# A decoder with cross-attention on one core: the context's low parts and the residual input by adding DMA transfers, and each slot's context projection moved to the front of its step

## The reference

```python
# x: 16 x 112 x 256 (from the first part), y = ctx_1024: 16 x 375 x 256, H = 16 heads of D = 16
q = softmax(_heads(x @ Wq.T + bq), axis=-1)
k = softmax(_heads(y @ Wk.T + bk), axis=-1)
v = _heads(y @ Wv.T + bv)
k_cumsum = sum(k, axis=-2, keepdims=True)
D_inv = 1.0 / sum(q * k_cumsum, axis=-1, keepdims=True)
kv = einsum('bhnd,bhne->bhde', k, v)
out = q + einsum('bhnd,bhde->bhne', q, kv) * D_inv
out = out.transpose(0, 2, 1, 3).reshape(x.shape[0], x.shape[1], C)
return out @ Wp.T + bp
# around it:
x = _layernorm(x + L0_attn(x, ...))      # first part; this sum is what the attention part begins with
x = _layernorm(x + L0_xattn(x, ctx_1024, ...))
x = _layernorm(x + L0_ffn(x, ...))
```

## Time and profile before

| | |
|---|---|
| Median of 3 runs | 1837.98 us (1837.52 to 1838.78) |
| The profiled execution's own time | 1839.21 us |
| Its span in the profile | 1837.5 us |
| Busy: PE, DVE, ACT, POOL | 1736.6 us (95%), 1242.6 (68%), 977.0 (53%), 3.6 |
| Attention part | from about 700 us to about 905 us |
| PE busy, and TensorE clock granted, 700 to 718 us | 14.39 of 18.00 us, 0.87 |
| the same, 718 to 743.4 | 22.28 of 25.40 us, 0.77 |
| the same, 743.4 to 792 | 45.40 of 48.60 us, 0.99 |
| the same, 792 to 836.4 | 39.47 of 44.40 us, 1.00 |
| the same, 836.4 to 872.9 | 33.13 of 36.50 us, 1.00 |

### The profile page before, as it was taken

One profiled execution on the slowest core, in us unless ns is written; L12 is line 12 of the kernel. 1 busy time (PEld: TensorE's weight loads), 2 busy tenths in 40 slices (PEclk: granted clock), 3 DMA queues, 4 the chain that ended last, 5 costly groups with the idle time before them and its releaser, 6 DMA issues.

```text
span 1837.5 us, 27225 instructions
## 1 busy us (share of the span) xinstructions
PE 1736.6 (95%) x10508; PEld 1520.3 (83%) x10508; DVE 1242.6 (68%) x1918; ACT 977.0 (53%) x1505; POOL 3.6 (0%) x26
## 2 busy tenths in 40 slices
PE   3599999999999998998999999999999999999997
PEld 1378888778888788888899889998999989999896
DVE  7999999999999855888554445444454544445446
ACT  4688898898989773444533333333333332333323
POOL 0000000000000000000000000000000000000000
PEclk9799999999999998999999999999999999999999
DMA  4000010001000002111111010000011001120001
GB/s 143 1 25 17 12 47 18 7 8 62 1 12 29 0 30 89 44 55 45 55 35 35 1 35 35 34 33 2 34 34 34 11 23 34 34 74 0 1 1 41
DMA packets 34702, 56.59 MB, mean 31 GB/s; under 512 B 3030, under 2 KB 20412, under 8 KB 33596
## 3 DMA queue, kind: packets, MB, share of 16 engines
q1 hardware_dynamic: 34620, 55.47, 9.3%
HBM read 51.79 MB, written 3.67 MB: 30 GB/s over the span
## 4 chain that ended last, share of the span: by engine, by line
PE 70%; DVE 24%; ACT 3%; issue 2%; DMA 0%; SPq 0%; ACTq 0%; DVEq 0%
PE fbank L1935 33%; PE fbank L1957 17%; PE pair L839 5%; PE pair L799 4%; PE pair L824 3%; DVE kfl L421 2%; PE proj L1429 2%; PE pair L809 2%; DVE st L268 2%; DVE aa L370 1%; DVE bb L366 1%; DVE pp L352 1%; PE qbanks L1465 1%; PE pair L789 1%; DVE x L409 1%
## 5 line engine op out<-in xcount | busy, mean ns | idle before, releaser
L1757 DVE TENSOR_TENSOR hf<-sil,fbank 128x512 f32<-128x512 f32 (+1 forms) x256 | 158.8, 620 | 479.2 <-PE fbank L1935 407.5
L1862 ACT ACTIVATE sil<-fbank 128x512 f32<-128x512 f32 (+1 forms) x256 | 139.2, 544 | 615.1 <-PE fbank L1935 615.1
L1935 PE MATMUL fbank<-xh,wh 128*128 128x512 f32 (+1 forms) x1024 | 289.8, 364 | 1.2 <-ACT sil L1862 1.2
L1935 PE MATMUL fbank<-xl,wh 128*128 128x512 f32 (+1 forms) x1024 | 289.0, 363 | 0.0
L1935 PE MATMUL fbank<-xh,wl 128*128 128x512 f32 (+1 forms) x1024 | 288.9, 363 | 0.0
L1957 PE MATMUL fbank<-wl,hh 128*128 128x256 f32 x896 | 250.3, 279 | 0.0
L1957 PE MATMUL fbank<-wh,hh 128*128 128x256 f32 x896 | 250.2, 279 | 0.0
L1957 PE MATMUL fbank<-wh,hl 128*128 128x256 f32 x896 | 250.1, 279 | 0.0
L1935 PEld LDWEIGHTS fbank<-xl,wh 128*128 128x128 f32 x1024 | 184.6, 189 | 30.8
L1935 PEld LDWEIGHTS fbank<-xh,wl 128*128 128x128 f32 x1024 | 184.4, 189 | 30.4
L1935 PEld LDWEIGHTS fbank<-xh,wh 128*128 128x128 f32 x1024 | 180.5, 189 | 27.8 <-ACT sil L1862 1.6
(11 more groups left out here) (239 smaller groups left out, 3109.6 us busy)
## 6 DMA issues: line engine op xcount, KB each, us to landing
raw<-in_w_gate SPq DMA_DIRECT2D x16, 512.0 KB, 3.8
raw<-in_w_up SPq DMA_DIRECT2D x16, 512.0 KB, 4.7
raw<-in_w_down SPq DMA_DIRECT2D x16, 512.0 KB, 5.7
raw<-in_w_ck SPq DMA_DIRECT2D x4, 1024.0 KB, 4.8
raw<-in_w_cv SPq DMA_DIRECT2D x4, 1024.0 KB, 4.8
raw<-in_ctx_t SPq DMA_DIRECT2D x4, 750.0 KB, 5.9
ct<-in_ctx_t SPq DMA_DIRECT2D x4, 750.0 KB, 4.9
x<-in_x SPq DMA_DIRECT2D x4, 448.0 KB, 6.9
```

Source lines behind the costliest of these rows:

```text
L1757: dve.tensor_tensor(hf[i][:, 0:w], sil[i][:, 0:w], banks(e, t, f)[1][:, 0:w], ALU.mult).then_inc(hf_ready, 1)
L1862: act.activation(sil[f % 2][:, 0:w], banks(e, t, f)[0][:, 0:w], ACT.Silu).then_inc(sil_ready, 1)
L1935: ins = pe.matmul(banks(e, t, f)[k][:, 0:w], m[h][:, o:o + P], a[:, b, columns(c)], start=i == 0, stop=i == 3 * CB - 1)
```

## The change

- `ctl` is no longer made by DVE. ACT, behind each `high_context`, writes minus the high part into `ctl` (scale −1.0), and POOL issues a DMA transfer that adds the slot's context from device memory to it (`accum_op=ALU.add`). PE waits for that transfer (`ctl_in`).
- `add_input` on DVE is gone with the buffers `xin`. POOL issues four transfers that add the input to `x` in place; DVE's `input_stats` waits for them and takes the statistics.
- On PE, `project` is cut into `project_values` and `project_rest`. Both stand at the front of each step, ahead of the query projection, the output projection and the turns; the by-head products of `attend` stand between them at i = 0.
- On DVE at i = 0, `denominators` and `rsqrt` stand ahead of `k_normalise`.
- SP's next context load waits for `cth_ready` (the high part) in place of the low part. `kvbd` takes the place in memory that `xin` had.

```diff
@@ gpsimd (new) @@
+            def add_context(s):
+                pool.wait_ge(minus_ready, s + 1)
+                if s >= 2:
+                    pool.wait_ge(ctl_in[s % 2], 16 * (s // 2))
+                pool.dma_start(ctl[s % 2][:, :, 0:S], io["ctx_t"][:, :, s * S:(s + 1) * S].bitcast(F32R),
+                               accum_op=ALU.add).then_inc(ctl_in[s % 2], 16)
+            def add_input(c):
+                if c >= 2:
+                    pool.wait_ge(sum_in[c % 2], 16 * (c // 2))
+                pool.dma_start(x[:, c * G:(c + 1) * G, :], xv[:, c * G:(c + 1) * G, :], accum_op=ALU.add)\
+                    .then_inc(sum_in[c % 2], 16)
+            add_context(0)
+            add_context(1)
+            pool.wait_ge(g["x_done"], 2 * STEPS)
+            add_input(0)
+            for s in range(2, B):
+                add_context(s)
+                if s % 2 == 0 and s // 2 < GROUPS:
+                    add_input(s // 2)
@@ sync @@
-            load_x(0)
-            load_x(1)
...
-                sp.wait_ge(ctl_ready, CG * (j - 1))
+                sp.wait_ge(cth_ready, CG * (j - 1))
                 load_context(sp, io, ct, ct_in, j)
-                if j * CG % G == 0 and j * CG // G >= 2:
-                    c = j * CG // G
-                    sp.wait_ge(sum_done, c - 1)
-                    load_x(c)
@@ vector @@
-            def low_context(s):
-                c0 = (s % CG) * S
-                dve.wait_ge(cth_ready, s + 1)
-                if s >= 2:
-                    dve.wait_ge(proj_done, s - 1)
-                dve.tensor_tensor(ctl[s % 2][:, :, 0:S], ct[s // CG % 2][:, :, c0:c0 + S], cth[s % 2][:, :, 0:S],
-                                  ALU.subtract).then_inc(ctl_ready, 1)
...
-            def add_input(c):
-                dve.wait_ge(xin_in[c % 2], 16 * (c // 2 + 1))
-                dve.tensor_tensor(chunk(c), chunk(c), xin[c % 2][:], ALU.add).then_inc(sum_done, 1)
-                dve.wait_ge(sum_done, c + 1)
+            def input_stats(c):
+                dve.wait_ge(sum_in[c % 2], 16 * (c // 2 + 1))
                 stats(1, c)
...
                     if i == 0 and c1 is not None:
-                        add_input(c1)
+                        input_stats(c1)
+                    if i == 0 and c2 is not None:
+                        denominators(c2)
+                    if i == 0 and c1 is not None:
+                        rsqrt(1, c1)
...
                     k_normalise(n)
-                    if n + 2 < B:
-                        low_context(n + 2)
-                    if i == 0 and c1 is not None:
-                        rsqrt(1, c1)
-                    if i == 0 and c2 is not None:
-                        denominators(c2)
@@ scalar, high_context @@
                 act.activation(cth[s % 2][:, :, 0:S], ct[s // CG % 2][:, :, c0:c0 + S], ACT.Copy).then_inc(cth_ready, 1)
+                act.wait_ge(cth_ready, s + 1)
+                act.activation(ctl[s % 2][:, :, 0:S], cth[s % 2][:, :, 0:S], ACT.Copy, scale=-1.0).then_inc(minus_ready, 1)
@@ tensor @@
             for n in range(B):
                 i, c1, c2 = stage(n)
+                if n + 1 < B:
+                    project_values(n + 1)
+                if i == 0 and c2 is not None:
+                    attend(c2)
+                if n + 1 < B:
+                    project_rest(n + 1)
                 if i == 1 and c1 is not None:
                     pe.wait_ge(xt_ready, c1 + 1)
                     tokens_out(qbanks, xt, wq, 1, q_done)
...
-                if n + 1 < B:
-                    project(n + 1)
-                if i == 0 and c2 is not None:
-                    attend(c2)
```

More of the change, by code:

```diff
@@ L928, in attention_phase @@
         x, ident = g["x"], g["ident"]
-        xin = [sb(f"xin{i}", [T, G, C]) for i in range(2)]
+        kvbd = sb("kvbd", [P, 2 * G, CB, P])
         q = [sb(f"q{i}", [T, G, C]) for i in range(2)]
@@ L945, in attention_phase @@
         top, total, rec = (sb(n, [ST, STILES * H]) for n in ("top", "total", "rec"))
-        kvbd = sb("kvbd", [P, 2 * G, CB, P])
         kcm = sb("kcm", [P, 2 * G, CB, P // D])
@@ L972, in attention_phase @@
         wkvh_ready, wkvl_ready = sem("wkvh_ready"), sem("wkvl_ready")
-        cth_ready, ctl_ready = sem("acth_ready"), sem("actl_ready")
+        cth_ready, minus_ready = sem("acth_ready"), sem("minus_ready")
+        ctl_in = [sem(f"actl_in{i}") for i in range(2)]
         v01_done, v2_done, proj_done, kv_done = sem("v01_done"), sem("v2_done"), sem("proj_done"), sem("kv_done")
@@ L977, in attention_phase @@
         bd_ready = sem("bd_ready")
-        xin_in = [sem(f"xin_in{i}") for i in range(2)]
-        sum_done = sem("sum_done")
+        sum_in = [sem(f"sum_in{i}") for i in range(2)]
         lnstat, lnlog, lny0, shift_ready = ({i: sem(f"{n}{i}") for i in (1, 2)}
@@ L987, in attention_phase @@
         dve_step = sem("adve_step")
-        g["sum_done"], g["v01_ready"], g["karg_ready"] = sum_done, v01_ready, arg_ready
+        g["num_done"], g["v01_ready"], g["karg_ready"] = num_done, v01_ready, arg_ready
         TURNS = (2 * G + 2, 3 * G + 2)
@@ L1014, in gpsimd @@
                                pattern=[[D, P // D], [0, D]], channel_multiplier=-1).then_inc(mask_set, 1)
+            xv = io["x"].rearrange("b t c -> t b c")
+            def add_context(s):
[17 more added lines that the diff above has]
+                    add_input(s // 2)
         def sync(sp):
-            xv = io["x"].rearrange("b t c -> t b c")
-            def load_x(c):
-                sp.dma_start(xin[c % 2][:], xv[:, c * G:(c + 1) * G, :]).then_inc(xin_in[c % 2], 16)
             sp.wait_ge(g["wo_done"], STEPS)
@@ L1036, in sync @@
             for j in range(2, B // CG):
-                sp.wait_ge(ctl_ready, CG * (j - 1))
+                sp.wait_ge(cth_ready, CG * (j - 1))
                 load_context(sp, io, ct, ct_in, j)
-                if j * CG % G == 0 and j * CG // G >= 2:
-                    c = j * CG // G
-                    sp.wait_ge(sum_done, c - 1)
-                    load_x(c)
             for c in range(GROUPS):
                 if c == 2:
-                    sp.wait_ge(ctl_ready, B - CG)
+                    sp.wait_ge(cth_ready, B - CG)
                     load_half(sp, g["raw"][1], io, 0, 1, g["raw_in"][1])
@@ L1212, in begin @@
                 dve.tensor_tensor(wkvl[:], wkv, wkvh[:], ALU.subtract).then_inc(wkvl_ready, 1)
-                low_context(0)
                 dve.wait_ge(const_set, 4)
@@ L1217, in begin @@
                 split_rows(0, 2)
-                low_context(1)
             def groups():
@@ L1422, in add_bias, with context_tile, project_values @@
                 return pe.matmul(out, onesr[:, 0:tokens], bias[:, j, :], start=False, stop=True)
[L1424 to L1434, removed]
+            def context_tile(s, out, t, cols):
+                n = 0
+                for a, w in ((cth, wkvh), (cth, wkvl), (ctl, wkvh)):
+                    for b in range(CB):
+                        ins = pe.matmul(proj[0:ST, out, :], a[s % 2][:, b, t * ST:(t + 1) * ST], w[:, b, cols],
+                                        start=n == 0, stop=n == 3 * CB - 1 and cols.start > 0)
+                        n += 1
+                return ins if cols.start else add_bias(proj[0:ST, out, :], 0, ST)
+            def project_values(s):
+                pe.wait_ge(ctl_in[s % 2], 16 * (s // 2 + 1))
                 if s:
@@ L1440, in project, with project_rest @@
                 for t in range(2):
-                    ins = tile(STILES + 1 + t, t, slice(C, 2 * C))
+                    ins = context_tile(s, STILES + 1 + t, t, slice(C, 2 * C))
                 ins.then_inc(v01_done, 1)
+            def project_rest(s):
                 if s:
@@ L1446, in project @@
                     pe.wait_ge(arg_ready, s)
-                tile(STILES, 2, slice(C, 2 * C))
+                context_tile(s, STILES, 2, slice(C, 2 * C))
                 if s == 0:
                     pe.wait_ge(bias_ready, 1)
-                tile(2, 2, slice(0, C)).then_inc(v2_done, 1)
+                context_tile(s, 2, 2, slice(0, C)).then_inc(v2_done, 1)
                 for t in range(2):
-                    ins = tile(t, t, slice(0, C))
+                    ins = context_tile(s, t, t, slice(0, C))
                 ins.then_inc(proj_done, 1)
@@ L1523, in tensor @@
             pe.wait_ge(const_set, 4)
-            project(0)
+            project_values(0)
+            project_rest(0)
             pe.wait_ge(w_in, 32)
@@ L1687, in gpsimd @@
         def gpsimd(pool):
-            pool.wait_ge(g["sum_done"], GROUPS)
+            pool.wait_ge(g["num_done"], GROUPS)
             pool.memset(eps[:], EPS).then_inc(eps_set, 1)
```

## The result

The changed kernel takes 1851.1 us (median of 4 runs, 1851.0 to 1854.1) where the kernel before takes 1838.3 (4 runs, 1837.5 to 1838.8): 1.0076 times as long, 95% interval 1.0064 to 1.0089. It is slower, as forecast, and within the range, but by 12.8 us and not by 5.4. The profiled execution has a span of 1849.3 us against 1837.5, so 11.8 of the 12.8 can be looked for in the two traces.

A forecast was written before the change was run, and what follows sets the result against it. PE, busy 95% of the span, was taken to bound the kernel. Order 1.3, slot 5 1.5, slot 9 0.45, input 0.5 and clock 1.7 gave +5.45 on the median 1838.0: 1843.4 us, range 1833 to 1852.

The forecast's parts named there:

- Waits for `xt`, −7.0: On PE before query and output projections: all seven waits for ACT's copy are covered, 7.0 us less.
- R waits for DVE's k, 0.9 each at steps 2, 6, 10, 14: On PE, the projection's rest after the values waits for k arguments queued behind DVE's query arguments, about 0.9 us each.
- rival D: The projection's rest never waits for DVE, so the 7.0 us mostly stay won: −6, 1832 us; chance 0.18.
- The walk of the order: Attention part, engine by engine: DVE's slot 4 k arguments end at 2.0 us; whole order 1.05 earlier with free transfers.
- The first group, walked alike, gains nothing: First group of attention steps: covered waits are eaten by slot 3's projection rest, 1.8 us behind the query arguments.
- L: Time from ACT's negative to the adding transfer's landing: 4.2 us for even slots, 5.2 for odd.
- my own sign of being wrong: Forecast is wrong if a slot's transfer takes under 3 or over 6 us to land.
- rival C: Adding transfers are slow, 6.2 and 7.2 us to land: +16.4, 1854 us; chance 0.17.
- rival B: Adding transfers land like plain ones, 3.3 us throughout: +2.1, 1840.1 us, not to be told from no change; chance 0.20.
- Slot 12, 2.35 for the order and 1.7 for the clock: PE waits 5 to 7 us before slot 12's values projection; lower clock behind it adds 1.7.
- Slots 5 and 9, 1.5 and 0.45: Before the values projections of slots 5 and 9: transfers land later than the slack allows, costing 1.5 and 0.45 us.
- Input, 0.5: First input chunk shares the DMA engines with 1.5 MB of weights: 0.5 us later, chosen between 0 and 2.

The follow-up runs named there:

- the order alone: Kernel before, with the change's new orders on PE and DVE but low parts and input still added on DVE: 1843.7 us, ratio 1.0032.
- five edits: The order alone plus slot 12's high part first, values' copy first, k normalised first, x turned early, next k arguments ahead of query arguments: 1827.7 us, ratio 0.9948.
- the mended kernel that adds: Changed kernel, adding transfers kept, with slot 12's high part first, values' copy first, k normalised ahead of the reciprocals: 1842.4 us, ratio 1.0035.
- adding at its best: Changed kernel with all five edits, adding transfers kept, context loads held until the odd slot's adding transfer has landed: 1830.6 us, ratio 0.9959.
- the mended order without adding: The order alone, with slot 12's high part first, values' copy first, k normalised ahead of the reciprocals: 1838.1 us, ratio 0.9992.

## Why the prediction was right in direction and too small in size

- **Waits for `xt`, −7.0**: right, all seven are gone.
- **R waits for DVE's k, 0.9 each at steps 2, 6, 10, 14**: right; 0.82, 0.98, 0.40, 0.98 us, so rival D's condition was rightly found unmet. But that they cost what they last is not shown: when they were taken away, KV waited longer by as much.
- **The walk of the order, "k arguments of 4 to 2.0"**: this step failed. It let DVE begin when R was over. But `k_arguments` also waits for ACT's values' copy, and ACT's queue had to be walked past the copy of the turned queries, which the change moves. The k arguments begin 2.6 us late, the block diagonals with them, and the by-head products wait 1.0 in steps 4, 8 and 12 with the order alone, in 4 and 12 in the changed kernel (in step 8 V(9)'s wait hides it). From KV(4) to KV(8) I had 40.2; the order alone takes 41.5, the changed kernel 41.9.
- **"The first group, walked alike, gains nothing"**: wrong at KV(0), which I did not walk. DVE's rsqrt, now ahead of k, waits for the statistics to come back from ACT: 4.6 us in the order alone, 3.0 when it is put back. Less lower clock from 718 to 743 us (0.90 against 0.77) seems to have paid this back (the turn of step 4 begins at 747.88, 748.35 in the walk). In all the order alone is +5.9, where the walk had it 1.05 earlier with harmless transfers; not all of the 7 is the walk's, since this kernel keeps the low parts on DVE.
- **L, 4.2 even and 5.2 odd**: mis-sized. It is 5.4 and, behind a load, 5.9 to 7.7. By my own sign of being wrong, a landing of over 6 us, six of the sixteen transfers fail. The plain part was right (3.3 expected, 3.5 measured), and the fixed 0.3 from the negative to the issue was missing. Doubling the moving part gave 0.9 for adding, where it costs 1.5; and a load beside it costs 0.5 to 2.3, where I had 1.0. Most of these values lie between my forecast and rival C.
- **The fit of the Trainium skill** (page "DMA: Bandwidth & Descriptors", section "Anatomy of one DMA — SWDGE (gpsimd) path"), which gives 2.9 us as an estimate for this size: the traces do not agree, as the plain transfers of POOL land in 3.5 to 3.7. The adding ones, which the fit does not speak of, land in 5.0 to 5.2, and with that rival B falls.
- **Slot 12, 2.35 for the order and 1.7 for the clock**: the place and the kind were right, the wait 7.6 (5 to 7 forecast), the clock 2.3. Taking it away wins 7.7. Of the 3.65 beyond my 4.05, L accounts for 1.2 and the clock for 0.6. From KV(8) to KV(11) the two traces differ by 6.6 (40.3 against 33.8), so some 1.1 of the other 1.8 lies outside this place; I can't assign it.
- **Slots 5 and 9, 1.5 and 0.45**: V(5) waits 0.2, for ACT, and V(9) 2.0. Behind V(5) the by-head products wait for the block diagonals anyway, which hides its transfer: moving the values' copy showed 1.8 there. V(9)'s transfer was later than I had it (L 6.7). That the two add up to 2.2 where I had 1.95 is luck.
- **Input, 0.5**: 5.0 before KV(0) against 3.0, of which the order makes 1.6. In the kernels that add it, the chunk landed 5.7 to 10.7 us after its issue; a single number was the wrong kind of answer here.

So the forecast took the right case and sized it too small, by two causes: an engine's queue that the walk left out, and a transfer that is 1.2 us longer at the one place where it counts as a wait and in part again as clock. Where most of the miss lies they weigh alike. From KV(8) to KV(12) the forecast has 48.25 (44.2, 2.35 and 1.7) and the changed kernel 52.1; of these 3.8, L and the clock are 1.8, and another 1.8 lie between KV(11) and KV(12) (11.7, by the walk 9.9), where DVE's k arguments again begin 2.6 us behind R(12).

## What to carry to other kernels

When work is moved on one engine, walk the queues of all engines past it, also those that only copy: each `wait` of a moved instruction names another queue whose order was made for the old place. Before giving work to a transfer, look for the one use with the least cover between issue and need; the sum of what the engine is relieved of says nothing about it. And an order can be mended place by place from the list of PE's waits: five edits of a few lines won 16.0 us over the order alone (13.3 of it in waits, from 25.5 to 12.2), while relieving DVE of 18.6 us, with the same order mended, was worth 2 to 3 less than its transfers cost. Read the granted clock beside the waits: an edit that only moves waits can come out shorter by a stretch of lower clock that is or isn't there.

## What the runs showed of the hardware

- A transfer that adds to SBUF, 375 KB issued by POOL, lands in 5.0 to 5.2 us alone, a plain one over the same queue in 3.5 to 3.7, one over SP in 3.5. Beside a plain load of 750 KB the adding one lands in 5.6 to 7.4, the plain one in 4.5 to 6.3; beside 1.5 MB the adding one in 8.4.
- In the stretch from 700 to 870 us of the changed kernel the adding queue moves 7.21 MB in 28.1% of the DMA engines' time, the other 8.69 MB in 16.3%: 2.1 times as long for a byte. Not all of this is adding: with the context transfers plain over the same queue, the same 7.21 MB take 19.7%.

```profile
q0 software_dynamic: 5664, 7.21, 28.1%
q1 hardware_dynamic: 4848, 8.69, 16.3%
```

- POOL's instruction for an adding transfer of 375 KB takes 1.1 us, for a plain one 0.7. Whether this is part of the 1.5 us by which the landing is later, no run shows.
- Kernels with transfers that are due soon mostly scatter more. The runs of the kernel before lie 4.1 us apart (1835.6 to 1839.7 over all comparisons), those of the mended kernel that adds 10 (1840.8 to 1851.0). The cause is not shown, and there are exceptions both ways: 3.5 us for adding at its best, 7.8 for the mended order without adding.
- With the order mended and no transfer to wait for, two heaps of runs 5 us apart differ in the mean granted clock by 0.003. Why it drops in some executions of one program and not in others stays open.
